# Scores and the search of batch 2 moved into the causal attention of layer 1

## The chip, the cores and the metric

The kernel runs on one core of one Trainium2 chip. The metric is the device time of one execution, in microseconds (us). Engines: PE is TensorE (matrix products), DVE is VectorE, ACT is ScalarE, POOL is GpSimd, SP is SyncE, which here issues DMAs. TensorE's clock is granted at one of two levels, 2.4 and 1.2 GHz; a granted clock of 1.00 is the first, 0.50 the second.

## The reference

A decoder of four layers works on `x`, 8 batches of 128 tokens by 128 features. Each layer adds three parts to `x`, each computed from the normalised `x`: a self attention, a cross attention, and a feed-forward part. The change lies in two parts of layer 1.

The causal attention (16 heads of 64):

```python
wei = jnp.einsum('hbqd,hbkd->hbqk', q, k) * hs ** (-0.5)
wei = jax.nn.softmax(jnp.where(causal, wei, -jnp.inf), axis=-1)
out = jnp.einsum('hbqk,hbkd->hbqd', wei, v).reshape(b, t, h * hs) @ proj_w.T + proj_b
```

The cross attention that follows (4 heads of 32; keys from a context of 128 tokens by 96 features). Each query keeps its 32 best keys; the mean over heads of the softmaxed weights makes `c_t`, which scales and shifts ("film") the input and the output of a state space model; that one is a convolution along the tokens with one kernel ("taps") for each feature:

```python
scores = jnp.where(vision_mask[:, None, None, :], scores, -jnp.inf)
topv, topi = jax.lax.top_k(scores, K_TOP)            # K_TOP = 32
probs = jax.nn.softmax(topv, axis=-1)
attn = jnp.zeros_like(scores).at[bi, hi, ti, topi].set(probs)
c_t = jnp.einsum('btg,bgd->btd', attn.mean(axis=1), V) * text_mask[..., None]
x = layernorm(x_text, g_norm_in, b_norm_in)
scale_in, shift_in = jnp.split(c_t @ W_film_in + b_film_in, 2, axis=-1)
x = x * (1.0 + mod_gate * scale_in) + mod_gate * shift_in
y = s4d(x, log_dt, A_re, A_im, C_re, C_im, D_skip)
```

## The kernel before

Each part of a layer is one block (or two); inside a block every engine has a program of its own, written out by hand, and semaphores order them. At a block's end all engines meet. P = 128, D = 128, B = 8; a bank is 512 fp32 columns of PSUM, and there are eight (`ps[0]` to `ps[7]`).

**The causal attention**, `layer_l1_attn` (L2136), runs in turns n = -6 to 16. A turn of 0 to 15 handles eight heads of one batch's rows (two turns for a batch). In turn n TensorE transposes the probabilities of n (L2339), projects queries, keys and values of a later pair of batches while there are any left (turns to 9), makes the scores of n + 2 (L2375, L2379), and multiplies the transposed probabilities of n with the values (PV, L2395) into O_BANKS[n % 2]. ScalarE makes the exponentials of n + 1 (L2463) and then empties PV's bank (L2490). VectorE copies the transposed probabilities to SBUF (L2556), inverts the sums (L2561) and takes the maxima of n + 2 (L2602); POOL scales the probabilities of n + 1 (L2253). In turns 4, 8, 14 and 16 a pair of batches is finished: the output product of 64 matmuls (L2353), ScalarE's bias (L2474), two transposes (L2407), a copy (L2497) and POOL's addition to `x` (L2267).

In these turns parts of the next block are made ahead. `BestKeys` (L2092) holds the search: `one_round` (L2116) takes, for each of four heads, the eight largest scores (MAX8) and replaces them in a copy by the lowest number (MATCH_REPLACE8); four rounds find 32. Which rounds stand in which turn is in the table `ROUNDS`. Batches 0 and 1 are scored and searched in turns 6 to 14. The pair of batches 2 and 3 has its measure (mean and variance) in turn 14; in turn 16 its rows are normed (L2526), transposed (L2303), copied, and the queries made (L2401); its keys are made in turn 15, those of batches 4 to 7 in turn 16 (L2297, `next_keys`). After turn 16 TensorE scores batch 2 (L4023, L4026).

**The best-key attention**, `top_attention` (L4030), is the next block. Per batch: TensorE's scores, ScalarE's copy of them to SBUF (`copy_scores`, L4251), VectorE's four rounds, ScalarE's exponentials of all scores (`exps`, L4240) and of those left over (`exps_left`, L4230) with their sums, POOL's difference and weight of the two (L4115, L4104 to L4106, L4118: the batch is then "kept"), TensorE's transposes summed over the heads (L4184), ScalarE's copy (L4257), a product with the values (L4193), a copy (L4261), the film product (L4197) and four ScalarE operations on it (L4219, L4221), and POOL's application of it (L4123 to L4130). The last batch's weights and film are done by VectorE (L4308 to L4317). VectorE's search starts with batch `FIRST` = 2; three slots hold scores (`SLOTS`). POOL also begins the inputs `u`: the norm's rstd, and `begin_inputs` with three operations of 128x512 for each half of the batches (L4096 to L4099), done ahead of batch 2. `keep_clock_bf(bank, n)` (L134) is n matmuls whose result nobody reads: eight after the queries (L4166), six at t = 7, five ahead of the last batch's transposes, four at the end.

SP: the next layer's weights (3.7 MB) are issued ahead of the block (L4776), then the taps go to DRAM (L4071), and, once they are there, eight transfers bring them back as shifted rows (`toe`, L4077), 1 MB each. The convolution (`state_space_out`, L4358) needs `toe` and the inputs of all batches.

## Time and profile before

| what | us |
|---|---|
| median of 3 runs | 1181.59 (1180.98 to 1185.31) |
| the profiled execution, its own time | 1178.47 |
| its span, first to last instruction | 1176.7 |
| PE, DVE, ACT, POOL busy over the span | 1065.6, 673.5, 557.6, 461.4 |
| mean granted clock of TensorE | 0.974 |

The profiled execution is 3.1 us shorter than the median of the timed ones. Times within the trace count from the span's start. A line of the timeline gives the start, the time from the first to the end of the last of the instructions that it puts together, the engine, the line of the kernel, and in brackets how long the engine had been idle and what released it.

### The profile page before, as it was taken

To read this page: it belongs to the slowest core of one execution; us is meant where nothing else is said; L and a number is where in the kernel's file an instruction comes from. 1 tells how busy PE (TensorE), PEld (TensorE's weight loads), DVE (VectorE), ACT (ScalarE), POOL (GpSimd) and SP (SyncE) were. 2 spreads that over 40 slices of the span, in tenths; PEclk is the share of its full clock that TensorE was granted. 3 is DMA by queue.
4 is the path that set the end of the run, shared out by engine and by line. 5 is a ranking of instruction groups with operands and counts; after the bars stand their busy time and mean duration, and the time that the engine had idled before them with its cause. 6 is when DMAs were issued, how large, how long until landed. Compare 5 with 4: busy or idle time off the path is not lost. (4 is left out here: it accounts for less than half of the span.)

```text
span 1176.7 us, 22941 instructions
## 1 busy us (share of the span) xinstructions
PE 1065.6 (91%) x8781; PEld 765.7 (65%) x8797; DVE 673.5 (57%) x2055; ACT 557.6 (47%) x1473; POOL 461.4 (39%) x545
## 2 busy tenths in 40 slices
PE   6999989899997689898999899978899999988996
PEld 5876858567674355676677566745567776666684
DVE  5555562445767846885678467638823117766512
ACT  5434334266575844355445455506543334653432
POOL 7968913123245943783487250012000004041423
PEclk9999999899998799999999999999999999999999
DMA  5000060232205801000000030000021100010312
GB/s 168 1 1 5 2 232 1 94 105 73 73 2 205 216 2 46 1 1 1 1 2 1 1 76 2 2 5 33 1 81 36 36 19 17 2 41 2 130 48 77
DMA packets 55084, 54.18 MB, mean 46 GB/s; under 512 B 19472, under 2 KB 45840, under 8 KB 53952
## 3 DMA queue, kind: packets, MB, share of 16 engines
q1 hardware_dynamic: 54048, 50.84, 14.0%
q0 software_dynamic: 928, 1.88, 0.5%
q8 instruction: 71, 1.16, 0.4%
q14 instruction: 37, 0.30, 0.1%
HBM read 44.08 MB, written 8.63 MB: 45 GB/s over the span
## 5 line engine op out<-in xcount | busy, mean ns | idle before, releaser
L482 POOL TENSOR_TENSOR ln_rstd<-ln_ve,ln_half 128x4 f32<-128x4 f32 x25 | 25.4, 1018 | 251.7 <-DVE ln_ve L457 251.7
L652 DVE TENSOR_REDUCE scratch<-bank 128x4 f32<-128x512 f32 x96 | 63.3, 684 | 31.2 <-PE bank L557 18.1
L1311 ACT ACTIVATE scratch<-bank 128x512 f32<-128x512 f32 x64 | 38.2, 596 | 66.2 <-PE bank L1267 66.2
L713 ACT ACTIVATE scratch<-bank 128x512 f32<-128x512 f32 x96 | 55.5, 597 | 23.4 <-PE bank L572 23.0
L2253 POOL TENSOR_TENSOR scratch<-scratch 128x512 f32<-128x512 f32 x32 | 33.3, 1040 | 82.7 <-DVE scratch L2561 82.6
L1330 DVE SCALAR_TENSOR_TENSOR x_res<-bank,scratch,x_res 128x128 f32<-128x128 f32 x64 | 18.0, 344 | 82.1 <-PE bank L1277 82.1
L1277 PEld LDWEIGHTS bank<-weights,scratch 128*128 128x128 f32 x512 | 59.5, 192 | 7.2 <-issue 7.2
L572 PE MATMUL bank<-ident,scratch 128*128 128x128 f32 x384 | 56.8, 278 | 7.9 <-ACT scratch L707 6.0
L3378 POOL TENSOR_TENSOR scratch<-scratch 128x16 f32<-128x16 f32 x16 | 50.6, 3163 | 33.4 <-DVE scratch L3774 24.9
L1267 PE MATMUL bank<-xnT,weights 128*128 128x512 f32 x128 | 59.2, 606 | 0.7 <-ACT xnT L1300 0.7
L1277 PE MATMUL bank<-weights,scratch 128*128 128x128 f32 x512 | 59.6, 275 | 0.0
L572 PEld LDWEIGHTS bank<-ident,scratch 128*128 128x128 f32 x384 | 42.6, 141 | 20.3 <-ACT scratch L707 8.4
L659 DVE TENSOR_TENSOR scratch<-bank,scratch 128x512 f32<-128x512 f32 x72 | 47.2, 683 | 0.8
L2463 ACT ACTIVATE scratch<-bank,scratch 128x128 f32<-128x128 f32 x128 | 45.0, 386 | 4.1 <-DVE scratch L2602 4.0
L3994 POOL TENSOR_TENSOR scratch<-scratch 128x1024 f32<-128x1024 f32 (+5 forms) x48 | 42.9, 894 | 3.8
L3989 POOL TENSOR_TENSOR scratch<-scratch 128x2048 f32<-128x2048 f32 x8 | 36.2, 4524 | 17.3 <-DVE weights L1870 16.9
L1267 PEld LDWEIGHTS bank<-xnT,weights 128*128 128x128 f32 x128 | 23.7, 196 | 24.7 <-issue 23.8
L1595 ACT ACTIVATE scratch<-bank 128x512 f32<-128x512 f32 (+1 forms) x44 | 22.7, 524 | 34.9 <-PE bank L1507 33.6
L3601 ACT ACTIVATE scratch<-bank 128x512 f32<-128x512 f32 x32 | 19.2, 599 | 40.4 <-PE bank L3415 40.4
L3036 POOL TENSOR_TENSOR scratch<-weights,xnT 128x128 f32<-128x128 f32 x8 | 3.4, 428 | 84.9 <-DVE weights L3252 84.9
L134 PE MATMUL bank<-key_bias,ident_bf 128*128 128x512 bf16 x115 | 33.9, 412 | 2.4 <-ACT weights L4275 1.1
L3415 PE MATMUL bank<-weights,xnT 128*128 128x512 f32 x64 | 31.8, 616 | 3.5 <-DVE scratch L3707 1.6
(645 smaller groups left out, 2913.7 us busy)
## 6 DMA issues: line engine op xcount, KB each, us to landing
scratch<-conv_kernels SPq DMA_DIRECT2D x8, 1024.0 KB, 11.2
weights<-e_l_ffn_w SPq DMA_DIRECT2D x20, 256.0 KB, 2.9
scratch<-e_l_ffn_w SPq DMA_DIRECT2D x4, 1024.0 KB, 15.2
values<-scratch SPq DMA_DIRECT2D x8, 512.0 KB, 2.7
scratch<-values SPq DMA_DIRECT2D x8, 512.0 KB, 4.3
weights<-w_l_ffn SPq DMA_DIRECT2D x1, 3698.0 KB, 11.6
scratch<-e_l_ffn_w SPq DMA_DIRECT2D x4, 768.0 KB, 6.9
weights<-w_l_attn SPq DMA_DIRECT2D x1, 2560.5 KB, 9.2
```

Source lines behind the costliest of these rows:

```text
L134: self.nc.tensor.matmul(self.ps[bank][:, :], self.ident_bf[:, :], self.key_bias[:, 0:BANK], start=True, stop=True)
L572: t = self.nc.tensor.transpose(self.core.ps[4 + n % 2][:, i * P:(i + 1) * P], self.shift[:, n % 4, i * P:(i + 1) * P], self.core.ident[:, :])
L652: self.nc.vector.tensor_reduce(self.top[:, n % 4, :], self.by_head(self.core.ps[n % 4][:, :]), AX_X, ALU.max, negate=True).then_inc(self.t ...
L659: self.nc.vector.tensor_tensor(self.by_head(self.shift[:, n % 4, :]), self.by_head(self.core.ps[n % 4][:, :]), self.top[:, n % 4, :].unsqu ...
L713: self.nc.scalar.activation(self.prob_of(n), self.by_head(self.core.ps[4 + n % 2][:, :]), ACT.Exp, scale=scale) \
L1267: nc.tensor.matmul(ps[UP_BANKS[i]][:, :], wa[e % 2][:, i * P:(i + 1) * P], core.xnT[:, half(h)], start=True, stop=True).then_inc(up_made.s ...
L1277: mm = nc.tensor.matmul(ps[Y_BANKS[u % 3]][:, t * P:(t + 1) * P], hT[h][:, i, t * P:(t + 1) * P], wb[e % 2][:, i, :], start=(i == 0), stop ...
L1311: nc.scalar.activation(hT[u % 2][:, i, :], ps[UP_BANKS[i]][:, :], act_func) \
L2463: a = nc.scalar.activation(prob[:, r, 4 * i + j, :], score_bank(n + 1, i)[:, j * P:(j + 1) * P], ACT.Exp, bias=top[:, r, 4 * i + j:4 * i + ...
L3378: nc.gpsimd.tensor_tensor(rn_first[:, s + 2, :] if s + 2 < FIRST else rn, ss, power, ALU.pow) \
L3989: link(tt(prod, z, wa[:, a].unsqueeze(1).broadcast_to([P, R, 2 * N]), ALU.mult))
L3994: link(tt(out, prod[:, :, 0:h], prod[:, :, h:2 * h], ALU.add))
```

## The change

What it does:

- The measure of batches 2 and 3 moves from turn 14 to turn 9, its power on POOL to turn 10, the norming of the rows to turn 10, their transposes to turn 11, keys to turn 12, queries to turn 13. The three results go through the PV bank of the turn before, and VectorE empties it (ScalarE before).
- Batch 2 is scored by TensorE in turn 15, copied by ScalarE there, and searched by VectorE in turn 16 (`STEPS: (4,)`). After turn 16 TensorE scores batch 3.
- ScalarE's exponentials of batch 0, both kinds, move from the second block into turn 16.
- POOL begins the inputs of batches 0 to 3 in turn 15, those of 4 to 7 in the second block at t = 3.
- In the second block the search begins with batch 3; VectorE norms the rows of batches 4 to 7 after one round instead of two.
- Of the fillers, the eight after the queries and the five ahead of the last batch go, and six become three.
- The taps are stored by SP in the causal attention; the second block issues their rows first and then the next layer's weights.

```diff
+def begin_inputs(core, link, pool, search, u, g_in, b_in, h):
+    rows = slice(B // 2 * h, B // 2 * (h + 1))
+    var, rstd, part = search.var[:, rows], search.rstd[:, rows], u[:, rows, :]
+    every = lambda a: a.unsqueeze(1).broadcast_to([P, B // 2, D])
+    tt, ts = core.nc.gpsimd.tensor_tensor, core.nc.gpsimd.tensor_scalar
+    link(tt(var, core.ln_mv[:, rows, 1], core.ln_rstd[:, rows], ALU.mult))
+    link(tt(var, var, core.ln_rstd[:, rows], ALU.mult))
+    link(ts(var, var, 1e-5, None, ALU.add))
+    link(tt(rstd, var, core.ln_half[:, rows], ALU.pow))
+    link(tt(part, core.xn[:, rows, :], rstd.unsqueeze(2).broadcast_to([P, B // 2, D]), ALU.mult))
+    link(tt(part, part, every(g_in), ALU.mult))
+    link(tt(part, part, every(b_in), ALU.add))
...
-    ROUNDS = {6: (0, 0, 0, 1), 7: (0, 0, 2, 0), 8: (2, 0, 1, 0), STEPS - 2: (0, 0, 2, 0)}
+    ROUNDS = {6: (0, 0, 0, 1), 7: (0, 0, 2, 0), 8: (2, 0, 1, 0), STEPS - 2: (0, 0, 2, 0),
+              STEPS: (4,)}
...
+            sp.dma_start(core.conv_dram.ap(), core.conv_kp).then_inc(taps.sem, taps.up(16))
+            sp.wait_ge(taps.sem, taps.at(0, 16))
...
+                if n == 10:
+                    pool.wait_ge(ahead.eps.sem, ahead.half(ahead.eps, 0))
+                    nc.gpsimd.tensor_tensor(core.ln_rstd[:, 2:4], core.ln_ve[:, 2:4], core.ln_half[:, 2:4], ALU.pow)
...
+                if n == STEPS - 1:
+                    pool.wait_ge(*core.w_loaded["l1_xattn"])
+                    pool.wait_ge(ahead.rstd.sem, ahead.half(ahead.rstd, 0))
+                    pool.wait_ge(ahead.xn.sem, ahead.batch(ahead.xn, 3))
+                    pool.wait_ge(filled.sem, filled.at(place["yT", 2, 1]))
+                    begin_inputs(core, link, pool, search, inputs_at, g_in, b_in, 0)
...
+            def score_third():
+                some = slice(2 * P, 3 * P)
+                for n in range(2):
+                    if n:
+                        pe.wait_ge(headed.sem, headed.at(0))
+                    for i in range(2):
+                        h = 2 * n + i
+                        row = slice(32 * h, 32 * h + 1)
+                        nc.tensor.matmul(ps[S_BANKS[i]][:, n * P:(n + 1) * P], core.ones_bf[row, :], core.key_bias[row, some],
+                                         start=True, stop=False)
+                    for i in range(2):
+                        part = slice(64 * n + 32 * i, 64 * n + 32 * i + 32)
+                        m = nc.tensor.matmul(ps[S_BANKS[i]][:, n * P:(n + 1) * P], queries_next[part, some],
+                                             keys_next[part, some], start=False, stop=True)
+                    m.then_inc(headed.sem, headed.up())
...
+            def prepare_second_pair(n, out):
+                if n == 11:
+                    turn_rows(out, 2).then_inc(ahead.turned.sem, ahead.turned.up())
+                if n == 12:
+                    next_keys(0, out)
+                if n == 13:
+                    pe.wait_ge(x_out.sem, x_out.at(2))
+                    nc.tensor.matmul(out[:, 0:2 * P], wq_next, core.xnT[:, 2 * P:4 * P], start=True, stop=True) \
+                        .then_inc(queries_made.sem, queries_made.up())
...
                 if n == STEPS - 1:
-                    next_keys(0)
+                    pe.wait_ge(keys_out.sem, keys_out.at(0))
+                    pe.wait_ge(queries_out.sem, queries_out.at(0))
+                    score_third()
                 if n == STEPS:
-                    next_keys(1)
-                    pe.wait_ge(copied.sem, copied.at(2 * STEPS - 1))
-                    turn_rows(ps[T_BANKS[0]], 2).then_inc(ahead.turned.sem, ahead.turned.up())
+                    pe.wait_ge(third_copied.sem, third_copied.at(0))
+                    next_keys(1, ps[S_BANKS[1]])
+                if n in (11, 12, 13):
+                    pe.wait_ge(outs.sem, outs.at(n - 1))
+                    prepare_second_pair(n, ps[O_BANKS[(n - 1) % 2]])
...
+                    if n in (12, 13, 14):
+                        pe.wait_ge(*((x_out.sem, x_out.at(2)), (keys_out.sem, keys_out.at(0)),
+                                     (queries_out.sem, queries_out.at(0)))[n - 12])
...
                 if n == STEPS:
-                    next_keys(1)
-                    act.wait_ge(ahead.turned.sem, ahead.half(ahead.turned, 0))
-                    nc.scalar.copy(core.xnT[:, 2 * P:4 * P], ps[T_BANKS[0]][:, 2 * P:4 * P]).then_inc(x_out.sem, x_out.up())
+                    next_keys()
+                    act.wait_ge(search.negated.sem, search.negated.at(0))
+                    for h in range(4):
+                        a = nc.scalar.activation(search.e0[:, h, :], search.s[:, h, :], ACT.Exp, bias=search.nmax[:, 0, h:h + 1],
+                                                 accum_out=search.tot[:, 0, h:h + 1])
...
+                if n == 9:
+                    dve.wait_ge(added.sem, added.at(UNITS // 2 - 1))
+                    ahead.dve_measure(dve, 2, 4)
...
+                if n == 10:
+                    dve.wait_ge(ahead.rstd.sem, ahead.half(ahead.rstd, 0))
+                    rows_normed(2)
...
-    search = BestKeys(core, c, spare, 2)
+    search = BestKeys(core, c, spare, 3)
...
-            pe.wait_ge(queries_out.sem, queries_out.at(0))
-            core.keep_clock_bf(QUERY_BANK, 8)
+            score(4)
             for t in range(2, B + 2):
                 b = t - 2
                 open_film(b)
-                if b == LAST:
-                    core.keep_clock_bf(SCORE_BANKS[3], 5)
...
-                if t + 2 < B:
-                    score(t + 2)
+                if t + 3 < B:
+                    score(t + 3)
                 if t == LAST:
                     pe.wait_ge(copied.sem, copied.at(LAST - FIRST))
-                    core.keep_clock_bf(SCORE_BANKS[3], 6)
+                    core.keep_clock_bf(SCORE_BANKS[3], 3)
...
             copy_scores(FIRST)
-            exps(0)
-            copy_scores(FIRST + 1)
...
-            exps_left(0)
             exps(1)
             act.wait_ge(norm.turned.sem, norm.half(norm.turned, 1))
             nc.scalar.copy(core.xnT[:, half(1)], ps[TURN_BANK][:, :]).then_inc(x_out.sem, x_out.up())
+            exps_left(1)
             act.wait_ge(queries_made.sem, queries_made.at(0))
             nc.scalar.mul(qT[:, half(1)], ps[QUERY_BANK][:, :], K ** -0.5).then_inc(queries_out.sem, queries_out.up())
-            for t in range(FIRST, B + 3):
-                if t - 1 < B:
+            copy_scores(FIRST + 1)
+            for t in range(2, B + 3):
+                if FIRST <= t <= B:
                     exps_left(t - 1)
...
-            sp.dma_start(core.conv_dram.ap(), core.conv_kp).then_inc(taps.sem, 16)
-            sp.wait_ge(taps.sem, taps.base + 16)
             for n in range(D // CHN):
...
+            core.load_following(sp)
```

## Rows read from the trace of the kernel before

**Rows 1.** Busy time by stretches (engines in the order of the header)

```profile
core 0: us, PE busy (x) PEld busy (x) DVE busy (x) ACT busy (x) POOL busy (x), PEclk, DMA share, GB/s
340.30:344.60 4.30, 3.79 (x44) 2.83 (x42) 3.30 (x9) 3.39 (x17) 2.55 (x3) 1.00 0.01 4
354.30:362.20 7.90, 6.73 (x86) 5.09 (x84) 0.00 (x0) 2.82 (x7) 0.72 (x1) 1.00 0.01 2
362.20:409.00 46.80, 32.07 (x147) 16.68 (x150) 45.94 (x303) 36.04 (x160) 39.61 (x57) 0.71 0.92 264
```

**Rows 2.** Timeline of POOL, batches 1 to 3 of the second block

```profile
373.95 1.27 POOL L4115 TENSOR_TENSOR scratch<-scratch 128x512 f32<-128x512 f32 x1 [2.23 <-ACT scratch L4230]
...
377.93 1.04 POOL L4096 TENSOR_TENSOR scratch<-xn,scratch 128x512 f32<-128x512 f32 x1
...
384.84 1.27 POOL L4115 TENSOR_TENSOR scratch<-scratch 128x512 f32<-128x512 f32 x1
...
387.82 1.04 POOL L4118 TENSOR_TENSOR scratch<-scratch 128x512 f32<-128x512 f32 x1
...
390.24 1.27 POOL L4115 TENSOR_TENSOR scratch<-scratch 128x512 f32<-128x512 f32 x1
```

**Rows 3.** Timeline, the second block's end and the convolution's start

```profile
408.00 0.27 DVE L2129 MATCH_REPLACE8 scratch<-scratch 128x128 f32<-128x128 f32 x1
...
409.63 0.41 ACT L4230 ACTIVATE scratch<-scratch,weights 128x128 f32<-128x128 f32 x1
...
411.38 0.36 DVE L4308 TENSOR_TENSOR scratch<-scratch 128x4 f32<-128x4 f32 x1 [3.11 <-ACT scratch L4230]
...
413.41 0.38 ACT L4221 ACTIVATE scratch<-bank,weights 128x128 f32<-128x128 f32 x1
...
414.34 2.34 PE L134 MATMUL bank<-key_bias,ident_bf 128*128 128x512 bf16 x5
...
416.47 0.70 PE L4184 MATMUL bank<-ident,scratch 128*128 128x128 f32 x4
...
421.55 1.95 PE L4358 MATMUL bank<-scratch 128*8 128x128 f32 x64 [1.19 <-PEq L4067]
```

**Rows 4.** Timeline, the second block's start and SP's transfers

```profile
362.20 0.58 ACT L4251 COPY weights<-bank 128x512 f32<-128x512 f32 x1 [1.21 <-PEq L2226]
...
363.22 1.02 POOL L482 TENSOR_TENSOR ln_rstd<-ln_ve,ln_half 128x4 f32<-128x4 f32 x1 [1.43 <-DVE ln_ve L457]
364.39 0.20 POOL L4087 TENSOR_TENSOR scratch<-ln_mv,ln_rstd 128x8 f32<-128x8 f32 x1
...
371.68 0.60 ACT L4275 ACTIVATE weights<-bank 128x512 f32<-128x512 f32 x1 [2.16 <-PE bank L4166]
...
374.15 24.66 SPq L4077 DMA_DIRECT2D scratch<-conv_kernels  x8
```

**Rows 5.** Timeline, the causal attention's turns 13, 15 and 16

```profile
341.50 0.66 PE L2339 MATMUL bank<-ident,scratch 128*128 128x128 f32 x4 [0.51 <-POOL scratch L2253]
...
351.75 0.60 PE L2297 MATMUL bank<-ctxT_sb,weights 96*128 96x256 f32 x2
...
353.08 0.60 DVE L2526 TENSOR_SCALAR xn<-x_res,ln_mv,ln_rstd 128x128 f32<-128x128 f32 x2
...
355.28 0.38 PE L2303 MATMUL bank<-ident,xn 128*128 128x128 f32 x2
355.60 3.84 PE L2353 MATMUL bank<-scratch,weights 64*128 64x128 f32 x64
...
359.37 0.70 PE L2401 MATMUL bank<-xnT,weights 128*128 128x256 f32 x2
...
361.07 0.72 POOL L2267 TENSOR_TENSOR x_res<-x_res,scratch 128x256 f32<-128x256 f32 x1 [8.03 <-ACT scratch L2497]
```

**Rows 6.** TensorE at its lower clock: a stretch, and four transposes

```profile
400.00:401.00 1.00, 1.00 (x5) 0.66 (x3) 1.00 (x8) 1.00 (x6) 0.86 (x3) 0.50 1.15 290
...
381.34 1.06 PE L4184 MATMUL bank<-ident,scratch 128*128 128x128 f32 x4
```

More of the change, by code:

```diff
@@ L2100, in __init__ @@
         self.best0, self.best = c.take(H, 8), c.take(H, 8)
-        assert c.at <= SCRATCH - SLOTS * H * P
+        self.e0, self.tot, self.tot_left = spare.take(H, P), spare.take(2, H), spare.take(2, H)
+        self.var, self.rstd = spare.take(B), spare.take(B)
         kept = Carve(core.scratch)
-        kept.at = SCRATCH - SLOTS * H * P
-        self.left = kept.take(SLOTS * H, P)
+        kept.at = SCRATCH - (SLOTS + 1) * H * P
+        assert c.at <= kept.at
+        self.e_left0, self.left = kept.take(H, P), kept.take(SLOTS * H, P)
         self.tops, self.removed, self.negated = (core.count(n) for n in ("values_made", "removed", "negated"))
@@ L2177, in layer_l1_attn @@
             "attn_shifted", "attn_valued", "attn_outs", "attn_added", "chained", "keys_made", "keys_out",
-            "queries_made", "queries_out", "mean_out", "film_out", "attn_projected"))
+            "queries_made", "queries_out", "mean_out", "film_out", "attn_projected", "exped_left", "kept", "values_out", "inputs_ready", "differed"))
+    taps = core.count("taps_stored")
+    g_in, b_in = (Carve(core.beside_next.tensor[:, at:at + D]).take(D) for at in core.norm_in)
+    inputs_at = core.scratch[:, D * P + 2 * B * D:D * P + 3 * B * D].rearrange("p (b d) -> p b d", b=B)
     loaded = (loaded0, loaded1)
@@ L2430, in empty, with next_keys @@
                 a.then_inc(emptied.sem, emptied.up())
-            def next_keys(h):
-                some = (slice(2 * P, 4 * P), half(1))[h]
-                act.wait_ge(keys_made.sem, keys_made.at(h))
-                nc.scalar.copy(keys_next[:, some], ps[S_BANKS[h]][:, 0:some.stop - some.start]) \
-                    .then_inc(keys_out.sem, keys_out.up())
+            def next_keys():
+                act.wait_ge(keys_made.sem, keys_made.at(1))
+                nc.scalar.copy(keys_next[:, half(1)], ps[S_BANKS[1]][:, :]).then_inc(keys_out.sem, keys_out.up())
             def empty_ahead(kind, b=0):
@@ L2481, in _ @@
                 if n == STEPS - 1:
-                    next_keys(0)
-                if n == STEPS:
-                    act.wait_ge(queries_made.sem, queries_made.at(0))
-                    nc.scalar.mul(queries_next[:, 2 * P:4 * P], ps[T_BANKS[1]][:, 0:2 * P], 32 ** -0.5) \
-                        .then_inc(queries_out.sem, queries_out.up())
+                    act.wait_ge(headed.sem, headed.at(1))
+                    for x in range(2):
+                        a = nc.scalar.copy(search.s[:, 8 + 2 * x:8 + 2 * x + 2, :],
+                                           core.banks[:, 0:2 * BANK].rearrange("p (c k) -> p c k", c=2)[:, :, x * P:(x + 1) * P])
+                    a.then_inc(third_copied.sem, third_copied.up())
                 if 0 <= n < STEPS:
@@ L4043, in top_attention @@
     slot = lambda b, h: b % SLOTS * H + h
-    e, e_left = ([c.take(H, P) for _ in range(2)] for _ in range(2))
-    tot, tot_left, weight = c.take(2, H), c.take(2, H), c.take(H)
+    e, e_left = [search.e0, c.take(H, P)], [search.e_left0, c.take(H, P)]
+    tot, tot_left, weight = search.tot, search.tot_left, c.take(H)
     meanT, ctT = c.take(P), c.take(P)
     film_in = spare.take(2, P)
-    var, rstd = c.take(B), c.take(B)
     minus_one, last_weight = c.take(H), c.take(H)
```

120 lines of the change are left out of this document (62 added, 58 removed).

## The prediction, made before the changed kernel was run

> **What bounds the kernel now.** I read the page's table of slices first, then the busy time by stretches, then the timeline of each engine from 340 to 425 us, and last the waits of that stretch.
>
> The change touches two blocks that follow each other: the causal attention (to 362.2 us) and the cross attention that keeps the 32 best keys (362.2 to 421.5, where the convolution of the state space starts). In the last 7.9 us of the causal attention VectorE does nothing, while TensorE is busy for 6.73; inside its loop TensorE is busy 3.79 of a turn's 4.30 us, so there it is the engine without room [rows 1]. In the second block VectorE is busy 45.94 of 46.8 us [rows 1]: six searches, 7.3 us each, and 1.9 us of norms. It looks like the bound, and it isn't the last to end. POOL runs back to back from batch 2 on: that batch starts at 384.84, is kept at 388.86, and batch 3 starts at 390.24, so 5.40 a batch [rows 2]. VectorE's search ends at 408.27, yet ScalarE reaches the last batch's second exponentials at 409.63 only, since its means wait for POOL's kept batches [rows 3]. So VectorE and POOL are bounds 1.4 us apart, and both must be shortened.
>
> The end of the block is a chain of one batch. ScalarE's film of batch 5 ends at 413.79; TensorE opens the last batch's banks, then does five matmuls that only keep the clock (2.34 us), and starts the last transposes at 416.47; the convolution starts at 421.55, 5.08 us later [rows 3]. VectorE, which began the last batch's weighting at 411.38 after waiting 3.11 for ScalarE [rows 3], needs about 2.2 for its four short operations and has it ready by 413.6, so the fillers are on the path.
>
> **The causal attention, turns 9 to 13.** VectorE gains the measure of two batches (moved from turn 14), two rows normed (0.60 from the tail) and three copies of 256 columns that ScalarE used to make. Each stands at the end of a turn, ahead of the next turn's copies. By the row of two rows normed and by the free 1.0 us (4.30 less 3.30) of a turn [rows 1, 5] I cost them at nothing except where they push POOL's scaling: there about 0.5 us late in turn 12. Added one after another they would be at most 0.9 + 0.6 + 3 x 0.4 = 2.7.
> TensorE gains two transposes (0.38), one key product (0.60 for two, of which the second starts 0.25 after the first, so 0.5 of the engine) and one query product (0.70, some 0.6) [rows 5], 1.5 in all, and they stand between a turn's transposes and its scores, so in the chain. Some of the 0.51 that TensorE waits for POOL in an odd turn [rows 5] takes them in. Walking turns 11 to 14 by the rows, turn 11 ends 0.3 late, turn 12 1.2 (late scaling and keys together), and turn 14 1.1. I take +1.1; bounds +0.3 and 1.5 + 2.7 = 4.2.
> The waits of PV in turns 12 to 14 on the emptied bank are met before: the copy stands ahead of the turn's own copies on the same engine. Queued behind them is the turn's PV, and behind that ScalarE's copy and its next exponentials.
>
> **Its tail.** The two transposes at 355.28 go, and with them 0.3 before the output product at 355.60 [rows 5]. The query product at 359.37 was beside ScalarE's reading, so nothing. TensorE scores batch 2 in turn 15, where the key product (0.60) lay hidden until VectorE's copies ended at 353.08 [rows 5]. ScalarE gains two copies there, and in turn 16 eight exponentials of batch 0, 0.39 each, 3.1 us, after its copy of the keys: they start where the output product starts and that takes 3.84 [rows 5], so they just fit (cover gone: up to 0.5). POOL's first half of the inputs, 5.4 us, lies in its 8 us of waiting for the last addition at 361.07 [rows 5]. VectorE's search, 7.3 us, starts when the scores are copied, about 353.7 + 1.1 with the measure of batches 4 and 5 ahead of it, and ends at 362.3; the last addition then ends at 361.79 + 1.1 - 0.3 = 362.6. So the search is hidden, with 0.3 to spare. The block ends **0.8 later**, at 363.0 (bounds 0 and 4).
>
> **The second block, from its start.** POOL's first batch needed 11.75 us to start its second one (373.95 less 362.20), since ScalarE did batch 1's second exponentials after the query bank, which it awaited for 2.16 [rows 2, 4]. Now ScalarE does: a copy of scores (0.58 [rows 4]), two value copies, for which it waits until TensorE has the products, to +2.95, four exponentials at 0.39 to 4.5, xnT (0.6) to 5.1, the four second exponentials to 6.6. The xnT copy needs VectorE's four normed rows (1.2 by the 0.60 of two [rows 5]), which now follow one round of the search instead of two. Batch 1 starts at +6.6, 5.1 earlier, and takes 4.02.
> Then POOL's inputs: before, six operations took 384.84 - 377.93 = 6.91 [rows 2]. Now one half is three of them, 3.45, and its own four small ones, 0.9 and a power on 4 columns of 1.02 [rows 4], some 2.0 with gaps: 5.45, so 1.45 less. Batch 2 starts at +16.1 instead of +22.64: **6.5 earlier**. From there the period stays 5.40, if ScalarE keeps up: eight exponentials at 0.39, four film operations at some 0.4 and two or three copies are 5.3 to 5.8 a batch.
> VectorE has five searches, 38.8 us with norms, and ends at 401.8, some 2 us before ScalarE gets to it; 7.3 less there against 6.5 on POOL, so POOL and ScalarE are late next, and VectorE's cut gives only what POOL's gives.
> **The fillers.** Without the five at the last batch, the transposes follow the opened bank: 416.47 - 414.3 = **2.15 earlier** [rows 3]. The eight after the queries and three of six at batch 5's text also go; they lay in waits: nothing.
> The sum: block start +0.8, POOL's chain -6.5, fillers -2.15: -7.9 at full clock.
>
> **The clock.** With all its fillers the block already ran partly at 1.2 GHz (granted 0.50 from 400 to 401, 0.71 over the block), where four transposes take 1.06 instead of 0.70 [rows 1, 3, 6]. At half clock the last chain loses 0.4 (transposes), 0.3 (text) and 1.0 (film), and the convolution's first groups, TensorE-bound, about 1.8: 3.5 in all; if it stays up, nothing. I take 1.0, nearer to the low end, because today the last transposes and the convolution run at full speed (0.70 for four, 1.95 for 64 small products [rows 3]) with only short work between them.
> The Trainium skill, "TensorE: Matmul & The Clock Gate" (What's actually happening), says that the throttled clock is the default and that activity releases it. This speaks against taking fillers out and would make the whole 3.5 due. The trace agrees in one place: the five fillers took 2.34, and the transposes behind them ran in 0.70, not 1.06.
>
> **The taps.** The rows' issue ran from 374.15 for 24.66 us [rows 4], so to 398.8, behind their own store and the next layer's weights; they had landed well before the convolution at 421.55. Now they start at 363 and are issued by 388, the weights behind them, whose layer starts more than 30 us after the convolution. Worth nothing now and nothing at 413.6: unmoved, their last transfer, issued at 398.8 with 3.1 us of issue a piece (24.66 over 8), would still be in some us ahead. SP's queue has nothing else behind them.
>
> **Sum.** -7.9 + 1.0 = **-6.9**. Against the profiled execution, 1178.47: 1171.6. The timed runs lie higher, median 1181.59, 3.1 above it; so **1174.7**. Bounds: best 0 for the attention and no clock loss, -8.65 - some 1 if ScalarE's chain shortens with it; worst +4 - 8.65 + 3.5 = -1.2.
>
> **Rivals.**
> (a) The clock takes back half: all 3.5, so -4.4, 1177.2. For: low clock in most of the block, sixteen fillers fewer. Against: three fillers before the chain and the last four stay, and less time passes between its steps. 0.17.
> (b) ScalarE's loop is the bound once VectorE isn't: mean, four exponentials, text, film, four exponentials come to 6.6 to 7.2 us from a kept batch to the one after next, and POOL's two periods leave it 6.8. At 0.4 to 0.6 late for each of five batches, 2.5 is lost, and the rest stays: -6.9 + 2.5 = -4.4, 1177.2. For: the balance is this close. Against: POOL ran without gaps before. 0.12.
> (c) Slower: the search at the tail isn't covered. If the causal loop loses its 4.2 in full and the search starts only after the last output product has its bank (356 to 361 instead of 354.8), the block ends up to 7.3 + 4.2 = 11.5 later, against 8.65 - 3.5 = 5.2 won: +6.3, 1187.9. It decides from a start of the search past about 360. For: TensorE and ScalarE, which feed the scores, are full in the loop. Against: the scores need nothing that is made after turn 13. 0.05.
> (d) The change doesn't move the end, because batch 1's exponentials still wait for something else and POOL's second batch starts as before: only the fillers' 2.15 is won, and 0.8 lost: -1.35, 1180.2. For: that exponential is behind three other engines' work. Against: each of those is measured above. 0.08.
> My forecast: 0.58.
>
> **Range.** 0.5% is 5.9 us, about what a measurement of this kernel tells from no change. 1171 (bound of the forecast, -10) to 1180.5 (takes in (a), (b) and (d)). Faster by over 0.5%: nine tenths of the forecast, 0.52, and a quarter of (a) and (b), in all 0.60; slower: (c) and a little, 0.06; within: the rest, 0.34.
>
> **What would show it.** Right: the second block starts at 362.6 to 363.4; VectorE's search of batch 2 lies before it and its last one ends near 402; POOL's first subtraction of batch 2 is 16 us after the block's start; the last transposes follow their opened bank at once; convolution at 413 to 415. Wrong: turns 11 to 14 longer by over 2 us; a gap on POOL before batches 3 to 6; granted clock 0.50 at the convolution's start.

## The result, and the profile after

| | before | after |
|---|---|---|
| median of 4 runs each, us | 1181.28 | 1171.99 |
| lowest and highest, us | 1179.90, 1185.31 | 1169.74, 1174.04 |
| profiled execution (its span), us | 1178.47 (1176.7) | 1174.04 (1172.3) |

The ratio of the times is 0.9918, with a 95% interval of 0.9899 to 0.9938: the change takes away 9.3 us (7.3 to 11.9). The forecast was 1174.7 in a range of 1171.0 to 1180.5, so the time is in the range, 2.7 under the forecast.

The two profiled executions differ by 4.4 us only, and the reason lies outside the change. The expert stage of layer 0, whose code is the same, took 63.07 us in the trace of before and 66.11 in that of after, 3.0 more. Without it the traces differ by about 7.6 us: the causal attention block has +0.5 (142.61 to 143.12), the second block up to the convolution −8.09 (59.35 to 51.26); from the convolution to the next layer both take 36.56. The expectations below were compared with the second block's length, which agrees to 0.2 us in five traces of kernels that should not differ in it (51.26 to 51.44), where timing tells 2.

Busy time by stretches, kernel after: the tail of the causal attention, the second block as far as VectorE and POOL are both at work, and then a stretch around the last batch's transposes, the steps up to the convolution, and its first products (engines in the order of the header):

```profile
core 0: us, PE busy (x) PEld busy (x) DVE busy (x) ACT busy (x) POOL busy (x), PEclk, DMA share, GB/s
354.30:365.70 11.40, 9.00 (x119) 7.02 (x119) 10.41 (x65) 6.78 (x26) 6.33 (x10) 1.00 0.01 1
365.70:411.00 45.30, 32.70 (x139) 16.95 (x140) 40.73 (x259) 37.77 (x160) 39.32 (x62) 0.72 0.93 270
...
407.00:412.00 5.00, 4.16 (x14) 2.13 (x14) 2.03 (x5) 3.91 (x12) 3.08 (x7) 0.73 0.00 0
412.00:416.90 4.90, 2.67 (x11) 1.52 (x10) 0.58 (x2) 2.60 (x9) 1.33 (x3) 0.93 0.00 0
416.90:419.00 2.10, 2.06 (x66) 1.88 (x67) 0.00 (x0) 1.23 (x4) 1.44 (x2) 1.00 0.02 4
```

The first stretch begins some 3.5 us earlier in the kernel than the 7.9 us of [rows 1], in which VectorE did nothing; it is now busy for 10.41 of 11.4 us, POOL for 6.33. The granted clock of the second block is 0.72, against 0.71 before; it is 0.73 around the last batch's transposes (they themselves take 1.06, the time of the half clock) and 1.00 by the convolution.

The timeline of POOL, kernel after, batches 1 to 3 of the second block (start, length, engine, line, operation; in brackets the idle time and who ended it). It answers to [rows 2]:

```profile
372.39 1.27 POOL L4186 TENSOR_TENSOR scratch<-scratch 128x512 f32<-128x512 f32 x1 [0.80 <-ACT scratch L4296]
...
376.38 0.20 POOL L2095 TENSOR_TENSOR weights<-ln_mv,ln_rstd 128x4 f32<-128x4 f32 x1
...
381.84 1.09 POOL L4186 TENSOR_TENSOR scratch<-weights,scratch 128x512 f32<-128x512 f32 x1
...
387.07 1.27 POOL L4186 TENSOR_TENSOR scratch<-scratch 128x512 f32<-128x512 f32 x1
```

Count from the block's start, 365.68. Batch 1 begins at +6.71 (before +11.75), batch 2 at +16.16 (+22.64), and POOL has only half of the inputs between them (376.38 to 381.84: 5.46). Batch 3 begins 5.23 after batch 2, not 5.40. The first subtraction takes 1.09 in even batches now, and 1.27 in odd ones; before it took 1.27 in all.

The timeline of the block's start and of its end, kernel after; it answers to [rows 3, 4]:

```profile
365.68 0.58 ACT L4317 COPY weights<-bank 128x512 f32<-128x512 f32 x1 [1.27 <-PEq L2248]
...
404.18 0.27 DVE L2146 MATCH_REPLACE8 scratch<-scratch 128x128 f32<-128x128 f32 x1
...
406.00 0.43 ACT L4296 ACTIVATE scratch<-scratch,weights 128x128 f32<-128x128 f32 x1
...
407.77 0.34 DVE L4373 TENSOR_TENSOR scratch<-weights 128x4 f32<-128x4 f32 x1 [3.33 <-ACT scratch L4296]
...
408.98 1.78 PE L4263 MATMUL bank<-weights,scratch 128*128 128x512 f32 x2 [0.35 <-ACT scratch L4327]
410.55 0.63 PE L4224 MATMUL bank<-film_bias_bf,ones_bf 96*128 96x256 bf16 x2
...
410.98 1.06 PE L4250 MATMUL bank<-ident,scratch 128*128 128x128 f32 x4
412.39 0.64 PE L4259 MATMUL bank<-scratch 128*128 128x128 f32 x2 [0.36 <-ACT scratch L4323]
413.38 1.13 PE L4267 MATMUL bank<-weights,scratch 128*128 128x256 f32 x4 [0.36 <-ACT scratch L4327]
...
416.94 1.95 PE L4423 MATMUL bank<-scratch 128*8 128x128 f32 x64 [1.56 <-PEq L4150]
```

VectorE's last search ends at 404.45, 1.55 before ScalarE comes to the exponentials it is for (406.00), and VectorE then waits 3.33 for ScalarE. The last transposes follow the opened banks at once, but take 1.06 instead of 0.70; the convolution begins 5.96 after them (before: 5.08), at +51.26. In the kernel before, the same steps were these (the last bank's opening, the text product, the film product; the transposes and the convolution are in [rows 3]):

```profile
413.91 0.64 PE L4153 MATMUL bank<-film_bias_bf,ones_bf 96*128 96x256 bf16 x2
...
417.52 0.49 PE L4193 MATMUL bank<-scratch 128*128 128x128 f32 x2 [0.35 <-ACT scratch L4257]
418.36 1.13 PE L4201 MATMUL bank<-weights,scratch 128*128 128x256 f32 x4 [0.35 <-ACT scratch L4261]
```

So of the 0.88 that the steps behind the transposes are longer, 0.36 lies in the transposes and 0.15 in the text product. The film product takes 1.13 in both. The other 0.37 is the wait in brackets ahead of the convolution, where one block ends and the next begins: 1.19 before, 1.56 after, both at a granted clock of 1.00. It is not the clock's, and no run shows what makes it.

The timeline of the causal attention, kernel after: turn 12's transposes and the key product behind them, the end of the search, the last output product and the last addition, against [rows 5]:

```profile
339.80 1.25 PE L2396 MATMUL bank<-ident,scratch 128*128 128x128 f32 x8
340.89 0.60 PE L2344 MATMUL bank<-ctxT_sb,weights 96*128 96x256 f32 x2
...
364.44 0.27 DVE L2146 MATCH_REPLACE8 scratch<-scratch 128x128 f32<-128x128 f32 x1
...
364.55 0.72 POOL L2298 TENSOR_TENSOR x_res<-x_res,scratch 128x256 f32<-128x256 f32 x1 [3.19 <-ACT scratch L2563]
```

The moved products stand behind a turn's transposes, as expected. Turn 9 starts 2.95 later than in the trace of before (the expert stage's 3.0), turn 13 3.63 later, turn 15 also 3.63, the second block 3.48: the loop loses 0.7, the tail gives 0.15 back. The search runs from 357.30 to 364.71, and the last addition, which waits for ScalarE's copy of the last output, begins at 364.55.

### The profile page after: what moved, and what is told of

Its sections match the earlier page's. It is cut to its first block and busy times, and to the rows that moved or that the text cites. A ratio compares the mean times of both kernels' runs of the same rounds, so it can differ in the third digit from the quotient of the medians.

```text
span 1172.3 us, 22933 instructions
## 1 busy us (share of the span) xinstructions
PE 1065.7 (91%) x8781; PEld 765.5 (65%) x8781; DVE 674.8 (58%) x2058; ACT 556.9 (48%) x1471; POOL 461.6 (39%) x549
## 5 line engine op out<-in xcount | busy, mean ns | idle before, releaser
L2321 PE MATMUL bank<-xnT,weights 128*64 128x128 f32 x512 | 32.4, 277 | 2.6 <-DVE scratch L2643 1.0
## 6 DMA issues: line engine op xcount, KB each, us to landing
weights<-w_l_ffn SPq DMA_DIRECT2D x1, 3698.0 KB, 16.1
```

## The experiments

Each block length is from the second block's start to the convolution; after has 51.26, before 59.35. Ratios are to before, timed together with the kernel, and kernels that were timed together stand together: the first four, the next four, the last four. `taps_back` and `again` turned out as stand-ins for after in their groups.

**The five fillers and the others put back into after: fillers_back.**

```diff
+            core.keep_clock_bf(QUERY_BANK, 8)
...
+                if b == LAST:
+                    core.keep_clock_bf(SCORE_BANKS[3], 5)
...
-                    core.keep_clock_bf(SCORE_BANKS[3], 3)
+                    core.keep_clock_bf(SCORE_BANKS[3], 6)
```

> The changed kernel with its sixteen fillers restored: eight after batch 4's scores, six instead of three at t = 7, five ahead of the last batch's transposes. Theory (the fillers stood on the chain of the last batch): the convolution starts 1.5 to 2.2 us later than in the changed kernel, counted from the second block's start, and the time is 1.5 to 2 us longer. Rival (their removal costs the clock): granted clock in the block rises from 0.72 and gives back what they take, so the time stays within 0.5 us or falls.

Measured: 1186.25 against 1191.72, ratio 0.9955 [0.9939, 0.9970]; the block takes 52.61, 1.35 more. The timelines of POOL and TensorE, and TensorE's clock in the stretches that answer to those of after (the block starts at 361.53):

```profile
383.40 1.27 POOL L4186 TENSOR_TENSOR scratch<-scratch 128x512 f32<-128x512 f32 x1 [0.44 <-ACT scratch L4299]
...
399.16 2.76 PE L134 MATMUL bank<-key_bias,ident_bf 128*128 128x512 bf16 x6
...
407.47 0.39 PE L4224 MATMUL bank<-film_bias_bf,ones_bf 96*128 96x256 bf16 x2
407.70 1.25 PE L134 MATMUL bank<-key_bias,ident_bf 128*128 128x512 bf16 x5
408.78 0.60 PE L4253 MATMUL bank<-ident,scratch 128*128 128x128 f32 x4
...
414.14 1.95 PE L4426 MATMUL bank<-scratch 128*8 128x128 f32 x64 [1.57 <-PEq L4150]
```

```profile
404.20:409.20 5.00, 3.70 (x19) 1.81 (x17) 1.85 (x5) 4.12 (x14) 2.50 (x5) 1.00 0.00 0
409.20:414.10 4.90, 2.66 (x12) 1.37 (x10) 0.59 (x2) 2.61 (x9) 1.33 (x3) 1.00 0.00 0
```

The last transposes start at +47.25 instead of +45.30, 1.95 later, and the rest to the convolution takes 5.36 instead of 5.96: the fillers cost 1.95 and give back 0.60. What they give back there is clock (1.00 against 0.73 and 0.93), and most of it is in the four transposes, 0.60 against 1.06.

The 1.95 is not that of the five alone. The last bank is opened 1.07 later than in after (+45.94 against +44.87), and from there to the transposes it takes 1.31 instead of 0.43, 0.88 more. The 1.07 comes from the other fillers: POOL's batch 3 now waits 0.44 for ScalarE and begins 0.48 later, batch 6 0.55 later (+38.10 against +37.55), and the six at t = 7 take 2.76 where three took 0.81. So in the changed kernel the eight and the three are not in waits, and taking them out is a part of the gain. The block's 1.35 is a little less than the 1.5 to 2.2 expected.

**Only the five fillers taken out of before: before_no_five.**

```diff
-                if b == LAST:
-                    core.keep_clock_bf(SCORE_BANKS[3], 5)
```

> The kernel before, with only the five fillers ahead of the last batch taken out. Theory: the last transposes follow the opened bank, 2.1 us earlier at full clock, or 1.8 with those transposes at the lower clock; 1179.3 against 1181.3. Rival (clock): no gain, since the last chain and the convolution's first groups run at the lower clock, -0.5 to +1.

Measured: 1188.18, ratio 0.9976 [0.9966, 0.9987]; the block takes 58.10, 1.25 less. TensorE's timeline (start 364.48):

```profile
417.00 1.06 PE L4182 MATMUL bank<-ident,scratch 128*128 128x128 f32 x4
```

This is the trade of the five alone: the transposes start 1.75 earlier, from them to the convolution it takes 5.58 instead of 5.08, of which the transposes have 0.36, and net 1.25 is left.

**The taps stored and loaded where they were: taps_back.**

```diff
-            sp.dma_start(core.conv_dram.ap(), core.conv_kp).then_inc(taps.sem, taps.up(16))
-            sp.wait_ge(taps.sem, taps.at(0, 16))
...
+            core.load_following(sp)
+            sp.dma_start(core.conv_dram.ap(), core.conv_kp).then_inc(taps.sem, taps.up(16))
+            sp.wait_ge(taps.sem, taps.at(0, 16))
...
-            core.load_following(sp)
```

> The changed kernel with the taps' part undone: the next layer's weights first, then the store of the taps and its wait, then their rows, all in the second block. Theory (it is worth nothing): the rows are issued some 12 us later than in the changed kernel, by about 402.5, land before the convolution, and the time is equal within 0.5 us. Rival (the rows are late for a convolution that now starts earlier): TensorE waits for them at the convolution's start, +1 to +3.

Measured: 1183.44, ratio 0.9938 [0.9920, 0.9956]; the block takes 51.39. SP's transfer of the rows:

```profile
376.27 24.73 SPq L4159 DMA_DIRECT2D scratch<-conv_kernels  x8
```

Issued to 401.0, they were there before the convolution at 415.32, which waited for something else. The earlier load is worth nothing (51.39 against 51.26 and, for the unaltered kernel's second trace, 51.41).

**All eight inputs in the second block again: inputs_back.**

```diff
-                if n == STEPS - 1:
-                    pool.wait_ge(*core.w_loaded["l1_xattn"])
...
-                    begin_inputs(core, link, pool, search, inputs_at, g_in, b_in, 0)
...
-                    begin_inputs(core, link, pool, search, u, g_in, b_in, 1)
+                    for h in range(2):
+                        begin_inputs(core, link, pool, search, u, g_in, b_in, h)
```

> The changed kernel with POOL's first half of the inputs back in the second block, ahead of the second half. Theory (POOL's chain is the bound after the change): its seven operations, 5.4 us by the trace of the changed kernel, are on the path in full; batch 2 begins 21.6 us after the block's start instead of 16.2 and the time grows by 4.8 to 5.4. Rival (VectorE's search is the bound): VectorE had ended 1.5 us before its result was asked for, so the POOL chain has room, and the time grows by 0 to 2.

Measured: 1188.99, ratio 0.9974 [0.9961, 0.9988], 5.55 more than `taps_back` in the same group; the block takes 56.29, 5.03 more. POOL's timeline (start 365.73):

```profile
376.44 0.20 POOL L2095 TENSOR_TENSOR weights<-ln_mv,ln_rstd 128x4 f32<-128x4 f32 x1
...
381.93 0.20 POOL L2095 TENSOR_TENSOR weights<-ln_mv,ln_rstd 128x4 f32<-128x4 f32 x1
```

One half is 5.49. Two halves put batch 2 at +21.66, 5.5 later, and the convolution moves with it by 5.0, although VectorE has as little to do as in after. So the block ends by POOL's chain once the search of batch 2 is out of it.

**A round less in each search, in after and in before: three_rounds and before_three_rounds.** The edit is the same in both; each search finds 24 keys, not 32.

```diff
-    H, K, TOP = 4, 32, 32
+    H, K, TOP = 4, 32, 24
+    search.TOP = TOP
```

> The changed kernel with three rounds of the search instead of four for each of batches 3 to 7 (the fourth eight of the best keys are left out): 1.8 us less of VectorE a batch, 9 in all. Theory (after the change POOL and ScalarE are the bound): VectorE ends near 395 and the time stays within 0.7 us. Rival (VectorE is the bound): 5 to 9 us shorter.

> The kernel before with three rounds instead of four for each of batches 2 to 7 of the second block (the fourth eight are left out): 11 us less of VectorE. Theory (VectorE ended 1.4 us before ScalarE reached its result, POOL and ScalarE are the bound already before): 0 to 0.7 us shorter. Rival (VectorE, busy for 98% of the block, is the bound, and the change gains by the search that it takes out): 6 to 10 us shorter.

Measured: three_rounds 1172.80 against 1179.70, ratio 0.9933 [0.9916, 0.9951], block 50.91 (−0.35). before_three_rounds 1181.31, ratio 1.0010 [0.9997, 1.0022], block 59.35, to the hundredth that of before. VectorE's wait at the end of the second kernel, then of the first (before 3.11, after 3.33):

```profile
412.86 0.43 DVE L4309 TENSOR_TENSOR scratch<-scratch 128x4 f32<-128x4 f32 x1 [7.44 <-ACT scratch L4231]
```

```profile
407.21 0.33 DVE L4374 TENSOR_TENSOR scratch<-weights 128x4 f32<-128x4 f32 x1 [10.57 <-ACT scratch L4297]
...
416.01 1.95 PE L4424 MATMUL bank<-scratch 128*8 128x128 f32 x64 [1.19 <-PEq L4151]
```

VectorE was busy for 98% of the block before, and taking some 11 us of search from it (a quarter of six searches of 7.3; busy 35.34 of 46.8 us instead of 45.94) gave nothing: it came back as wait. Less work on VectorE can't by itself be what made the block shorter. The 0.35 of three_rounds is not the search's either: its last transposes start at +45.39, as in after (+45.30), and its wait ahead of the convolution is 1.19 instead of 1.56.

These runs do not show that the search could have stayed. In before it ended at +46.07, and in after ScalarE comes to its result at +40.32. With six searches in the block, of whose 46.8 us only 0.86 were idle, ScalarE would have waited there for about 5 us (an estimate from these rows): of the 7.1 by which it comes earlier, the slack of 1.4 and little more would have been left. POOL's relief without VectorE's was not run.

**The tail's search cut to one round: tail_one_round.** It leaves 24 of batch 2's best keys out.

```diff
-              STEPS: (4,)}
+              STEPS: (1,)}
```

> The changed kernel with one round instead of four in the tail of the causal attention (batch 2 keeps eight keys): 5.4 us less of VectorE there. Theory (the search is covered by the output product and POOL's last addition, 0.65 us to spare): the block's end does not move, time within 0.5 us. Rival (the search ends the block): 0.7 to 3 us shorter.

Measured: 1173.25, ratio 0.9934 [0.9919, 0.9949]; the causal block takes 143.14 (after 143.12). VectorE's search is over by 358.84, and POOL's last addition still waits as long for ScalarE:

```profile
364.12 0.73 POOL L2298 TENSOR_TENSOR x_res<-x_res,scratch 128x256 f32<-128x256 f32 x1 [3.19 <-ACT scratch L2563]
```

The search in the tail is covered, and costs the block's end nothing. The second block takes 50.93, 0.33 less, again with a wait of 1.20 instead of 1.56 ahead of the convolution.

**Batch 1's second exponentials after the query bank, as before: left_after_queries.**

```diff
-            exps_left(1)
...
+            exps_left(1)
```

> The changed kernel with ScalarE's second exponentials of batch 1 after its copy of the queries, as the kernel before had them. Theory (batch 1's start on POOL sets POOL's chain): ScalarE waits for the query product, batch 1 is 1.8 to 2.2 us later on POOL, and the time grows by as much. Rival (something later sets the chain): within 0.5 us.

Measured: 1173.40, ratio 0.9936 [0.9920, 0.9951]; the block takes 52.72, 1.46 more. ScalarE's and POOL's timelines (start 363.64):

```profile
370.22 0.60 ACT L4338 ACTIVATE weights<-bank 128x512 f32<-128x512 f32 x1 [1.56 <-PE bank L4235]
```

```profile
372.49 1.27 POOL L4186 TENSOR_TENSOR scratch<-scratch 128x512 f32<-128x512 f32 x1 [2.94 <-ACT scratch L4296]
```

ScalarE waits 1.56 for the query bank, and batch 1 starts at +8.85, 2.14 later. Batch 6 is still 2.12 later on POOL (+39.67), and of this 1.46 reaches the convolution. Behind it 0.54 is won back by the last transposes' start, where TensorE's film product ahead of the last bank runs at the full clock:

```profile
409.07 1.12 PE L4263 MATMUL bank<-weights,scratch 128*128 128x512 f32 x2 [0.35 <-ACT scratch L4327]
```

In after the same product took 1.78. The last transposes take 0.60 instead of 1.06, but TensorE then waits 0.83 for ScalarE's copy, and only 0.12 more is won. The timed runs don't show the 1.46: the ratio is that of three_rounds and tail_one_round, which don't have it. The order is worth about 2 of the 5.04 that batch 1 gained; the rest came with batch 0's exponentials having gone to the causal attention, which was not tried alone.

**The same kernel again: again.** It tests whether the timed 9.3 or the 7.6 of the traces is the change's.

> The changed kernel once more, unaltered, beside the kernel before on one chip. The traces put its gain at 8.1 in the second block less 0.5 in the causal attention, 7.6. Theory (the rest of the 9.3 first timed is scatter of four runs): 7 to 8 shorter than before, ratio 0.993 to 0.994. Rival (something outside the two blocks gains too): 9 or more.

Measured: 1183.16 against 1189.51, ratio 0.9951 [0.9937, 0.9965], −6.4 us; block 51.41, causal block 142.80. I had expected 0.993 to 0.994. The two intervals, 0.9899 to 0.9938 and 0.9937 to 0.9965, hardly meet, and the traces' −7.7 lies between.

**POOL relieved of one operation in each of seven batches: shift_later.**

```diff
-                    pool.wait_ge(film_out.sem, film_out.at(4 * b + 3))
-                    nc.gpsimd.tensor_tensor(shift_out[:, b, :], shift_out[:, b, :], core.xn[:, b, :], ALU.add)
...
+            nc.gpsimd.tensor_tensor(shift_out[:, 0:B - 1, :], shift_out[:, 0:B - 1, :], core.xn[:, 0:B - 1, :], ALU.add)
```

> The changed kernel with POOL's third film operation (0.41 us a batch, seven of them ahead of the last) taken out of the second block and done for seven batches at once where the convolution begins. Theory (POOL's chain and ScalarE's loop are bounds close together: ScalarE waited 0.79 twice and 0.35 once for POOL): POOL has 2.0 less before the last batch, ScalarE gives back a part, the convolution starts 0.8 to 1.6 earlier, counted from the block's start. Rival (ScalarE alone is the bound): within 0.3 us.

Measured: 1182.32, ratio 0.9944 [0.9930, 0.9959]; the block takes 51.44, nothing less. I had expected the period to shrink. POOL waits instead, and the timelines of ScalarE, TensorE and POOL show for whom; below them TensorE's clock during the film product:

```profile
391.33 0.27 ACT L4321 COPY scratch<-bank 128x128 f32<-128x128 f32 x1 [0.70 <-PE bank L4248]
393.04 0.24 ACT L4325 COPY scratch<-bank 128x128 f32<-128x128 f32 x1
...
396.73 0.27 ACT L4321 COPY scratch<-bank 128x128 f32<-128x128 f32 x1 [0.69 <-PE bank L4248]
...
393.34 2.07 PE L4261 MATMUL bank<-weights,scratch 128*128 128x512 f32 x2 [0.90 <-ACT scratch L4325]
...
395.63 1.06 PE L4248 MATMUL bank<-ident,scratch 128*128 128x128 f32 x4
...
396.18 1.27 POOL L4186 TENSOR_TENSOR scratch<-scratch 128x512 f32<-128x512 f32 x1 [0.54 <-ACT scratch L4294]
```

```profile
393.30:395.30 2.00, 1.96 (x3) 0.70 (x4) 2.00 (x15) 2.00 (x9) 1.77 (x4) 0.50 1.37 463
```

From one mean copy on ScalarE to the next it is 5.40: exponentials and the text's copy, then TensorE's film product at the half clock (2.07), the next bank opened (0.63), the next transposes (1.06), and again the mean copy. None of the steps shown waited for POOL, and the loop takes as long as POOL's own period. Rival (b) had a loop of this kind: it is a second bound, at the same height as the first, and so it cost nothing against the forecast.

**The exponentials' buffer moved: e1_beside, and both edits: best.** The odd batches' exponentials go into another tensor, so that the 1.27 subtraction has its input elsewhere.

```diff
+        self.inputs, self.tensor = c.tensor[:, 0:4 * SSM + 2], c.tensor
...
-    e, e_left = [search.e0, c.take(H, P)], [search.e_left0, c.take(H, P)]
+    e, e_left = [search.e0, Carve(core.ssm.tensor).take(H, P)], [search.e_left0, c.take(H, P)]
```

> The changed kernel with the exponentials of the odd batches in another buffer than those left over. In the changed kernel POOL's difference took 1.09 where its two inputs lie in two buffers and 1.27 where both are in one. Theory (the place of the inputs sets it): all seven at 1.09, and the convolution 0.3 to 0.6 earlier. Rival (something else in the odd batches): three stay at 1.27, no difference.

> The changed kernel with both: the third film operation later and the odd exponentials in another buffer. Theory: POOL 2.5 less ahead of the last batch, ScalarE's loop the bound by then; the convolution 1.0 to 1.8 earlier than in the changed kernel, time 1169 to 1171 on the chip where the changed one has 1172. Rival (ScalarE takes the bound at once): no more than the first of the two alone.

Measured: e1_beside 1182.61, ratio 0.9948 [0.9935, 0.9961]; best 1182.36, ratio 0.9943 [0.9927, 0.9958]; both blocks 51.41. POOL's subtractions in e1_beside, grouped (line, operation, count, shortest, median and longest in ns):

```profile
L4186 POOL TENSOR_TENSOR scratch<-weights,scratch x4: 1089/1091/1098, 365.8 to 401.3; 128x512 f32<-128x512 f32 x4
L4186 POOL TENSOR_TENSOR scratch<-ssm_sb,scratch x3: 1267/1268/1276, 370.4 to 395.8; 128x512 f32<-128x512 f32 x3
```

The odd ones take 1.27 still, with input and output in different tensors. What makes the difference of 0.18 is open. And `best` is no faster than `again`: none of these beats the changed kernel.

## Why the prediction was right

By its own steps, from the traces:

| step | forecast | measured |
|---|---|---|
| causal attention's end | +0.8 (loop +1.1, tail −0.3) | +0.5 (+0.7, −0.15) |
| POOL's batch 2 from the block's start | +16.1, 6.5 earlier | +16.16, 6.48 earlier |
| its batches after that | 5.40 each, 0 | 0.46 less over four |
| the five fillers | −2.15 | −2.03 (opened bank to transposes 0.43 for 2.56, −2.13) |
| the clock | +1.0 | +0.51 |
| the wait between the two blocks | 0 | +0.37 |
| taps | 0 | 0 |
| sum | −6.9 | −7.6 |

**The bound was named rightly.** VectorE's 98% busy time [rows 1] was not what the block waited for. The forecast read it off one number, VectorE's search ending 1.4 before ScalarE asks for it [rows 3], and before_three_rounds shows it: 0.00 for 11 us less work. Its other half, "both must be shortened", fits the rows too, since the slack of 1.4 is far less than the 7.1 by which ScalarE comes earlier; but POOL's relief alone was not run, so that half is worked out and not shown.

**POOL's chain** makes the gain. Batch 1 was forecast at +6.6 and came at +6.71; half of the inputs was put at 5.45 and took 5.46. inputs_back shows that 5.5 on POOL becomes 5.0 at the end, and left_after_queries that 2.14 becomes 1.46. Both pass to POOL's batch 6 in full (+5.53 and +2.12); a part is won back behind it, mostly where in both runs the film product ahead of the last bank took 1.12 or 1.13 instead of 1.78.

**The period.** The forecast's 5.40 came out as 5.35 on average: (403.23 − 381.84) / 4. The four periods of before were not all 5.40 either: one was 5.64, and they add up to 21.85; after has 21.39. The 0.46 is the largest mis-sized term of the sum. As far as the runs show, its reason lies in another term, "the eight after the queries and three of six also go; they lay in waits: nothing". With them back, fillers_back has 21.94, and POOL waits for ScalarE at batch 3. That POOL's subtraction takes 1.09 instead of 1.27 in every other batch, for which the trace of before had no row, is not enough: fillers_back has it too. So the fillers outside the last chain would be on the changed kernel's path, and all of them together are worth 1.07 by the opening of the last bank. Whether they lay in waits in the kernel before was not run. The sum's misses (0.46 here, 0.3 in the causal attention, 0.5 in the clock) all go one way; only the 0.37 between the blocks, which it didn't have, goes the other, so that it came out within 0.7 is in part luck.

**Fillers and clock** were to be weighed together, and were: −2.15 + 1.0 forecast, −2.03 + 0.51 measured, to which a wait of 0.37 between the blocks is added that the forecast didn't have. The near agreement of 1.0 with the whole 0.88 is luck. The five taken out of before alone gave −1.25, all the fillers put back into after 1.35. In after the granted clock was 0.73 from 407 to 412 and 0.93 up to the convolution. The film product ahead of the last bank took 1.78 instead of 1.50; that lies in the −2.03. Behind the opened bank the transposes lost 0.36 of the 0.4 allowed them, the text product 0.15 of 0.3, the film product nothing of 1.0 (1.13 in both traces), and the convolution's first 64 products nothing of 1.8 (1.95 in both). The Trainium skill, "TensorE: Matmul & The Clock Gate" (What's actually happening), has the throttled clock as the default, which spoke for the whole 3.5 of rival (a); the trace agrees in the direction, with fillers_back at 1.00 where after has 0.73, but at a seventh of that price (0.51 of 3.5), since the clock was back at 1.00 for the film product (from 413 us) and by the convolution.

**The rivals.** (a) and (d) are out by size. (c), the uncovered search, is out by tail_one_round. The search ended at 364.71, 0.6 before POOL's last addition did, so the margin of 0.3 was judged about right. (b) is right in that a loop through ScalarE bounds the block beside POOL, and it adds nothing to the time. It was put 0.4 to 0.6 a batch too long; by the rows of shift_later it is 5.40, as long as POOL's period, and 2.07 of it are a film product of TensorE at the half clock, which the rival's list has not.

**What stays open.** The timed gain was 9.3 the first time and 6.4 the second, the traces' is 7.6 and 7.7. The first interval (7.3 to 11.9) holds that, the second (0.0035 to 0.0063 of 1189.51, so 4.2 to 7.5) ends just short of it. How much of the 2.7 by which the median lies under the forecast is the change's is not settled; the traces give 0.7 of it. Open too are the wait of 1.19 or 1.56 between the blocks, and what POOL's relief would have given without VectorE's.

## What to carry to other kernels

A full engine need not be the bound: look for the last thing that the next stage waits for, and measure how long the full engine's result has lain ready by then. That slack, here 1.4, is also about all that can be won elsewhere before the full engine becomes the bound. Before one of two engines is relieved, work out the loop through the others; here POOL's chain and the loop of ScalarE and TensorE at the half clock both take 5.40 a batch, so relief of POOL alone bought nothing more. Fillers on the last chain are to be priced as the delay that they make less what the faster clock gives back there, here 1.75 less 0.50 for five (before_no_five). A filler that lay in a wait before a change has to be looked at again after it.

The next candidate would be the loop at the half clock: to open the film's bank after the transposes, or to keep the clock up during the film product. It wasn't tried.

## What the runs showed of the hardware

- **One stage without any change in it has two lengths, 10 us apart.** The same kernel, timed at 1171.99 the first time, took 1183.16 the second. SP's last transfers in the traces, from the last layer's tokens to its experts' results, kernel after first and `again` behind it:

```profile
1121.82 2.01 SPq L1449 DMA_DIRECT2D scratch<-rows_of_tokens  x4
1161.44 2.01 SPq L1455 DMA_DIRECT2D scratch<-rows_of_experts  x4
```

```profile
1118.87 2.01 SPq L1449 DMA_DIRECT2D scratch<-rows_of_tokens  x4
1169.39 2.01 SPq L1455 DMA_DIRECT2D scratch<-rows_of_experts  x4
```

It is 39.6 us against 50.5 between the two, 10.9 more in that stage; everything ahead of it was 2.95 earlier. All kernels that were timed together have the same of the two lengths: 39.0 to 39.9 in the first pair and the second four, 49.1 to 50.5 in the first four and the last four. The first four and the second four both carry the chip number 3 (the last four 8), so the number of the chip does not tell the length, and the reason is open. Only kernels that were timed together can be compared here.

- **A stage whose code nobody touched has more than one length.** Layer 0's experts took 63.07 us in two of the 14 traces (before, fillers_back) and 65.7 to 66.1 in the others; from 160 to 180 us the granted clock was 0.91 in before and 0.83 in after. A difference of two whole profiled executions can't be read without it.

- **Where one block ends and the next begins, the wait has two lengths.** Ahead of the convolution TensorE waited 1.19 to 1.20 us in five of the 14 traces (before, before_no_five, before_three_rounds, three_rounds, tail_one_round) and 1.56 to 1.57 in the other nine. The granted clock doesn't set it: fillers_back has 1.57 at 1.00.

- **The same subtraction on POOL takes 1.09 or 1.27 us**, steady to 0.01, in even and odd batches of after, whose exponentials lie in different buffers; in before it took 1.27 to 1.30 in all. Moving the odd batches' exponentials into another tensor did not change their 1.27.
